# A third bank pair for two sequences' scores, an earlier pair of feed-forward turns, and newly searched instruction orders in a four-block transformer kernel

## The chip, the cores and the metric

The kernel runs on one core of a Trainium2 chip. The core has a matrix engine (PE, TensorE; its weight loads are shown as PEld), a vector engine (DVE), an activation engine (ACT), a general engine (POOL, GpSimd) and a queue engine (SP) that only issues DMAs here. Each engine executes its own instruction list strictly in order and waits on semaphores for the others. Times are microseconds of device time of one execution.

## What is computed

Sixteen sequences of 512 tokens with 128 features pass four residual blocks, each on its layer-normed input: a selective scan, a mixture of eight experts, causal attention with 16 heads, and a feed-forward block.

```python
x = x + _L0_attn_ref(_layernorm(x), ...)   # scan: h = a_t * h + bx_t, 256 channels x 16 states
x = x + _L0_ffn_ref(_layernorm(x), ...)    # residual-norm gate, top 2 of 8 experts
x = x + _L1_attn_ref(_layernorm(x), ...)   # latent q, k, v; clip, causal softmax; 16 heads
x = x + _L1_ffn_ref(_layernorm(x), ...)    # silu(w1 x)*w2 x, gelu(h1), gelu(h2), w3
```

## The kernel before

There are two phases. **Phase one** pipelines the scan, the gate with its experts, and attention over the 16 sequences: while sequence b is scanned, its predecessor is in the experts and the ones before in attention. **Phase two** does the feed-forward block for all 16 sequences. Between them every engine waits for the last residual and for the last layer-norm factor (`phase_one_over`).

Work is written as small generators, the strands: `pe_scores(b)`, `dve_g_gate(b)`, `pool_masks(b)` and so on. A strand is cut into steps by `yield`. `in_order` merges all strands of an engine by a planned time for each step: `PERIOD * b + TIMES[name][k]`, in phase one with a shift from `EDGES` for the first three and the last three sequences. The tables only fix the order in which each engine meets its instructions; they delay nothing at run time. "scores15.4" below is step 4 of sequence 15 (the last one) in the strand `pe_scores`.

The parts that the change and the prediction touch:

- PSUM has eight banks of 512 fp32 columns. Bank 0 holds the scan's input, bank 1 the scan block's projections, bank 2 the attention projections, banks 3 and 4 (one pair) the gate and the experts, banks 5 and 6 (another pair) the attention scores, bank 7 the attention values.
- `pe_scores` has 20 steps a sequence. Each writes 128 x 1024 scores into a pair, and ACT's exponential (L1092) empties it into `prob`. With one pair PE may write step s only once ACT has emptied step s - 1. The last sequence uses both pairs in turn, since the experts no longer need banks 3 and 4 then.
- `pool_masks` zeroes the part above the diagonal (L1124) before `pe_values` multiplies with the values (L1145). `pe_t_proj` makes the attention projections (L931 to L956), `pool_t_proj` adds the two rotary parts (L1018), and `sp_rows` moves the rows to where the scores read them, with 16 DMAs a sequence in two halves (L412 to L421). `pe_t_out`, `dve_t_out` end attention (L1175, L1200).
- `dve_f_first`, `pe_f_first`, `act_f_first` prepare the feed-forward inputs of sequences 0 and 1 in phase one: normalise (L1689), turn on PE into bank 1 (L471), copy the high part (L1607), subtract for the low part (L1696). `dve_f_setup` scales two small vectors and copies the five weights to another fp32 form (L1451).

```python
def dve_f_first(self, general):
    yield from self.dve_f_setup(general)
    for b in range(2):
        yield from self.dve_f_norm(b, general)
```

## Time and profile before

| | us |
|---|---|
| median of 3 runs | 1606.09 (1604.8 to 1608.68) |
| the profiled execution, its own time | 1609.73 |
| its span, first to last instruction | 1608.2 |
| mean granted PE clock | 0.959 of full speed |
| PE busy in the span | 1474.6 |
| DVE busy in the span | 1354.4 |

A busy time is the union of an engine's instructions; a row of the timeline merges neighbouring instructions of one line, gives start, length and count, and in brackets how long the engine had been idle and what ended that.

### The profile page before, as it was taken

The page shows a single profiled execution, that of the slowest core. Times are in us where ns is not written, and L with a number is a line of the kernel's source. Part 1 is how long each engine was busy: PE and PEld are TensorE (multiplying, and loading weights), DVE is VectorE, ACT ScalarE, POOL GpSimd, SP SyncE. Part 2 cuts the span into 40 slices and gives each one's busy share as a digit, 9 for nine tenths or more (in the row PEclk, how much of TensorE's full clock was granted, in tenths as well). Part 3 has the DMA queues.
Part 4 walks back from the last instruction along what each step waited for, and adds up shares of the span by engine and source line. Part 5 has one row for each costly group of instructions (what it writes and reads, how often), then busy time and mean ns, then how long its engine had stood idle before and what let it go on. Part 6 is the DMA issues. An engine that isn't in the chain of part 4 may idle for free.

```text
span 1608.2 us, 23773 instructions
## 1 busy us (share of the span) xinstructions
PE 1474.6 (92%) x7687; PEld 789.1 (49%) x7687; DVE 1354.4 (84%) x2518; ACT 1242.6 (77%) x2144; POOL 1239.7 (77%) x1219
## 2 busy tenths in 40 slices
PE   4356799999999999999999999999989899999997
PEld 2123344444444444444444444434434688788885
DVE  5999899999999999999999999995431787977774
ACT  5875699999999999999999999995545555555542
POOL 4988799999999999999999999996232355555562
PEclk8676799999999999999999999999999899999999
DMA  4000000000000000000000000002000000000000
GB/s 157 1 0 0 20 1 21 4 18 21 1 20 5 17 12 10 20 1 21 5 17 21 1 21 4 17 15 79 21 11 10 1 1 14 14 14 14 8 20 29
DMA packets 14688, 27.59 MB, mean 17 GB/s; under 512 B 3981, under 2 KB 4566, under 8 KB 14042
## 3 DMA queue, kind: packets, MB, share of 16 engines
q1 hardware_dynamic: 14554, 25.98, 5.9%
q8 instruction: 62, 1.02, 0.3%
q14 instruction: 72, 0.59, 0.1%
HBM read 9.20 MB, written 4.19 MB: 8 GB/s over the span
## 4 chain that ended last, share of the span: by engine, by line
PE 45%; DVE 28%; ACT 16%; issue 5%; DMA 4%; POOL 1%; SPq 1%; ACTq 0%; DVEq 0%; POOLq 0%
DVE state_fast L634 14%; PE bank L1076 9%; PE bank L1569 7%; PE bank L1545 7%; ACT prob_fast L1092 5%; ACT state_fast L619 4%; PE bank L747 4%; DMA stacks_fast<-parts_fast 3%; PE bank L1145 3%; ACT bank L762 3%; PE bank L505 2%; DVE chan_all_kept L570 2%; PE bank L1589 2%; DVE own_fast L892 2%; PE bank L1518 2%
## 5 line engine op out<-in xcount | busy, mean ns | idle before, releaser
L634 DVE TENSOR_TENSOR_SCAN state_fast<-state_fast,bank 128x512 f32<-128x512 f32 x512 | 592.0, 1199 | 9.6 <-ACT bank L601 5.2
L658 POOL TENSOR_TENSOR sum_fast<-sum_fast,state_fast 128x512 f32<-128x512 f32 x384 | 480.4, 1275 | 11.2 <-DVE state_fast L634 11.1
L1092 ACT ACTIVATE prob_fast<-bank 128x1024 f32<-128x1024 f32 x320 | 325.4, 1018 | 94.7 <-PE bank L1076 80.2
L1076 PE MATMUL bank<-stacks_fast 64*128 64x512 f32 (+3 forms) x2048 | 365.1, 466 | 22.6 <-DMA stacks_fast<-parts_fast 13.4
L619 ACT ACTIVATE state_fast<-chan_all_kept,neg_a_fast 128x512 f32<-128x512 f32 x512 | 344.4, 713 | 9.1 <-POOL sum_fast L652 8.6
L1076 PEld LDWEIGHTS bank<-stacks_fast 64*128 64x128 f32 x2048 | 172.2, 187 | 217.6 <-ACT prob_fast L1092 107.1
L1124 POOL TENSOR_SCALAR_AFFINE_SELECT prob_fast<-prob_fast 128x512 f32<-128x512 f32 x256 | 169.4, 674 | 121.4 <-ACT prob_fast L1092 119.3
L1145 PE MATMUL bank<-prob_fast,v_ext_fast 128*32 128x512 f32 (+3 forms) x2048 | 172.5, 442 | 5.3 <-POOL prob_fast L1124 5.3
L1758 POOL TENSOR_TENSOR cell_a_fast<-th_fast,cell_a_fast 128x512 fp32r<-128x512 f32 x64 | 99.4, 1553 | 80.3 <-ACT cell_a_fast L1630 80.3
L747 PE MATMUL bank<-we_t_fast,xnt_g_fast 128*128 128x512 f32 x256 | 141.9, 651 | 2.8 <-DVE g_prod_fast L882 2.8
L714 PE MATMUL bank<-resid_m_fast,xnt_g_fast 128*128 128x512 f32 x256 | 133.8, 631 | 6.5 <-DVE gate_fast L798 5.1
L1545 PE MATMUL bank<-cell_a_fast,w_all_fast 128*128 128x512 f32 x512 | 129.1, 395 | 0.0
L1569 PE MATMUL bank<-cell_b_fast,w_all_fast 128*128 128x512 f32 x512 | 127.8, 393 | 0.0
L1545 PEld LDWEIGHTS bank<-cell_a_fast,w_all_fast 128*128 128x128 f32 x512 | 96.7, 189 | 21.9 <-issue 0.4
L1569 PEld LDWEIGHTS bank<-cell_b_fast,w_all_fast 128*128 128x128 f32 x512 | 96.0, 188 | 21.3
L1145 PEld LDWEIGHTS bank<-prob_fast,v_ext_fast 128*32 128x32 f32 x2048 | 48.5, 108 | 113.6 <-issue 95.7
L1704 DVE SCALAR_TENSOR_TENSOR th_fast<-th_fast,bank 128x512 f32<-128x512 f32 x64 | 43.8, 684 | 65.5 <-ACT th_fast L1624 65.5
L798 DVE TENSOR_REDUCE gate_fast<-bank 128x4 f32<-128x512 f32 x128 | 83.3, 679 | 17.9 <-ACT bank L762 17.7
L652 POOL TENSOR_TENSOR sum_fast<-state_fast 128x512 f32<-128x512 f32 x64 | 86.5, 1360 | 7.1 <-DVE state_fast L634 7.1
L1774 POOL TENSOR_TENSOR cell_c_fast<-full_fast,cell_c_fast 128x512 fp32r<-128x512 f32 x32 | 41.6, 1299 | 64.9 <-DVE cell_c_fast L1737 64.9
L1630 ACT ACTIVATE cell_a_fast<-th_fast 128x512 fp32r<-128x512 f32 x64 | 40.7, 635 | 64.1 <-DVE th_fast L1713 64.0
L1624 ACT ACTIVATE th_fast<-bank,s_half_kept 128x512 f32<-128x512 f32 x64 | 43.9, 687 | 55.8 <-PE bank L1518 55.7
(218 smaller groups left out, 2632.2 us busy)
## 6 DMA issues: line engine op xcount, KB each, us to landing
stacks_fast<-parts_fast SPq DMA_DIRECT2D x128, 64.0 KB
stacks_fast<-rest_fast SPq DMA_DIRECT2D x128, 32.0 KB
out_x<-f_out_fast SPq DMA_DIRECT2D x16, 256.0 KB, 2.0
x_res_kept<-in_x SPq DMA_DIRECT2D x1, 2048.0 KB, 14.3
chan_all_kept<-in_h_t SPq DMA_DIRECT2D x2, 1024.0 KB, 9.3
x_res_kept<-in_x SPq DMA_DIRECT2D x1, 1024.0 KB, 9.9
chan_all_kept<-in_w_t SPq DMA_DIRECT2D x3, 256.0 KB, 3.0
x_res_kept<-in_x SPq DMA_DIRECT2D x2, 256.0 KB, 3.3
```

The lines of the kernel that those rows point to most:

```text
L619: act.activation(self.state(b, i)[:], self.chan(b, ct)[1], ACT.Exp, scale=self.neg_a[:, i:i + 1]).then_inc(self.a_decay.sem)
L634: dve.tensor_tensor_scan(h[:], h[:], self.banks[0][:], 0.0, ALU.mult, ALU.add).then_inc(self.v_scan.sem)
L658: pool.tensor_tensor(part[:], part[:], self.state(b, i + 1)[:], ALU.add).then_inc(self.p_sum.sem)
L714: pe.matmul(banks[3 + half][:], xnt[:, k * P:(k + 1) * P], self.resid_m[:, half * 512:(half + 1) * 512], start=True, stop=True).then_inc(s ...
L747: pe.matmul(banks[3 + e % 2][:], xnt[:, k * P:(k + 1) * P], self.we_t[:, half * 512:(half + 1) * 512], start=True, stop=True).then_inc(sel ...
L1076: ins = pe.matmul(self.scores(b, step)[:, c:c + SEQ - P * kt], rows[:, 1, h // 2, P * kt:P * kt + P], rows[:, 0, h // 2, P * kt:SEQ], star ...
L1092: act.activation(self.probs[u % 2][:, i * 1024:(i + 1) * 1024], self.scores(b, 5 * g + n)[:], ACT.Exp, scale=SCALE).then_inc(self.a_prob.sem)
L1124: pool.affine_select(out=blocks, in_=blocks, compare_op=ALU.is_ge, fill=0.0, base=0, pattern=[[0, GROUP], [1, P]], channel_multiplier=-1). ...
L1145: ins = pe.matmul(bank[32 * j:32 * j + 32, P * kt:SEQ], v_ext[:, v:v + 32], self.probs[u % 2][:, c:c + SEQ - P * kt], start=(kt == 0 and g ...
L1545: ins = pe.matmul(banks[2 + mt % 2][:], w["h1_t"][:, c:c + P], self.f_a[s][k][:, i], start=(k + i == 0), stop=(k == MT - 1 and i == parts ...
L1569: ins = pe.matmul(banks[4 + mt % 2][:], w["h2_t"][:, c:c + P], self.f_h1[s][k][:, i], start=(k + i == 0), stop=(k == MT - 1 and i == parts ...
L1758: pool.tensor_tensor(cell[:, 1], th[:], cell[:, 0].bitcast(F32), ALU.subtract).then_inc(self.p_f_lo.sem)
```

## The change

1. Banks 0 and 1 become one tensor of 1024 columns, a third pair. Sequence 14 uses two pairs for its scores (5/6 and 0/1), sequence 15 all three (5/6, 0/1, 3/4). Each step waits for the exponential as many steps back as there are pairs. The first use of banks 0/1 also waits for the low part of feed-forward input 1, which is read from bank 1.
2. `dve_f_first` does the two normalisations first and `dve_f_setup` last, and the tables put the two turns right behind the scan block of sequence 15.
3. `TIMES`, `EDGES`, `PERIOD` and `F_PERIOD` are new, `EDGES` has six more numbers a strand (a stretch of the strand's steps), and the shifts hold in phase two as well. No instruction is added or dropped.

```diff
-PERIOD, F_PERIOD = 72369, 31463
+PERIOD, F_PERIOD = 72390, 35011
...
-def place(period, name, b, k, edges):
-    shift = EDGES[name][EDGE_OF[b]] if edges and name in EDGES and b in EDGE_OF else 0
-    return period * b + TIMES[name][k] + shift
+def place(period, name, b, k):
+    times, shift = TIMES[name], 0
+    if name in EDGES and b in EDGE_OF:
+        at = EDGE_OF[b]
+        shift = EDGES[name][at] + (times[k] - times[0]) * (EDGES[name] + [0] * 6)[6 + at] / 1000
+    return period * b + times[k] + shift
...
-        self.banks = [ctx.enter_context(nc.psum_tensor(f"bank{i}", [P, 512], F32)) for i in range(3)]
+        first = ctx.enter_context(nc.psum_tensor("bank0_1", [P, 1024], F32))
+        between = ctx.enter_context(nc.psum_tensor("bank2", [P, 512], F32))
...
+        self.banks = halves(first) + [between] + halves(self.doubles[0]) + halves(self.doubles[1]) + [last]
+        self.doubles.append(first)
...
-        return self.doubles[0 if b == NSEQ - 1 and step % 2 else 1]
+        return self.doubles[self.score_rooms(b)[step % len(self.score_rooms(b))]]
+
+    def score_rooms(self, b):
+
+        return {NSEQ - 2: (1, 2), NSEQ - 1: (1, 2, 0)}.get(b, (1,))
...
-                if b == NSEQ - 1 and step == 1:
+                step, rooms = 5 * g + n, len(self.score_rooms(b))
+                if step >= rooms:
+                    pe.wait_ge(self.a_prob.sem, self.a_prob.at(b, step - rooms))
+                elif step == 0 and b:
+                    pe.wait_ge(self.a_prob.sem, self.a_prob.at(b - 1, 19 if rooms < 3 else 18))
+                elif step == 1 and b == NSEQ - 2:
+                    pe.wait_ge(split.sem, split.at(1))
+                elif step == 1:
+                    pe.wait_ge(self.a_prob.sem, self.a_prob.at(b - 1, 19))
+                elif step == 2:
                     pe.wait_ge(self.v_g_acc.sem, self.v_g_acc.at(b, 15))
...
     def dve_f_first(self, general):
-        yield from self.dve_f_setup(general)
         for b in range(2):
             yield from self.dve_f_norm(b, general)
+        yield from self.dve_f_setup(general)
```

Merging the strands by the old and by the new tables gives the orders themselves. PE around the start of sequence 14's scores, before and after:

```
before: values13.12 scores14.0 t_proj14.5 scores14.1 g_own15.0 values13.13 scores14.2 g_own15.1 g_experts15.0 t_out13.0 scores14.3 values14.0
        ... scores14.6 g_experts15.4 values14.2 scores14.7 g_experts15.5 scores14.8 g_experts15.6 g_experts15.7 scores14.9
after:  values13.12 scores14.0 scores14.1 values13.13 g_own15.0 scores14.2 g_own15.1 scores14.3 g_experts15.0 t_out13.0 g_experts15.1
        g_experts15.2 scores14.4 g_experts15.3 g_experts15.4 values14.0 values14.1 g_experts15.5 g_experts15.6 scores14.5 t_out13.1 g_experts15.7
```

Behind that, and in sequence 15:

```
PE before:   scores15.3 t_out14.0 values15.0 scores15.4 t_out14.1 values15.1 scores15.5 scores15.6 values15.2 scores15.7 scores15.8 f_first15.0 scores15.9 values15.3
PE after:    scores15.3 scores15.4 t_out14.1 values15.0 values15.1 scores15.5 scores15.6 scores15.7 values15.2 scores15.8 scores15.9 scores15.10 values15.3
DVE before:  t_norm15.0 t_proj15.0 t_proj15.1 f_first15.0 (the setup) values14.0 ... values14.3 f_first15.1 f_first15.2 t_out14.0 f_moments14.0 f_first15.3 values15.0
DVE after:   s_out15.1 f_first15.0 s_out15.2 g_norm15.0 t_proj14.0 t_proj14.1 f_first15.1 f_first15.2 g_sums15.0 ... t_out14.0 f_moments14.0 f_first15.4 (the setup) values15.0
POOL before: masks14.8 masks14.9 t_proj15.0 masks14.10
POOL after:  masks14.8 t_proj15.0 masks14.9 masks14.10
```

In a middle sequence:

```
PE before:  g_experts8.0 g_own8.1 t_out6.0 scores7.3 values7.0 g_experts8.1 t_out6.1
PE after:   g_own8.1 g_experts8.0 t_out6.0 scores7.3 t_out6.1 g_experts8.1 values7.0
DVE before: scans9.31 s_norm12.0 g_experts8.0 g_experts8.1 t_out6.0 f_moments6.0
DVE after:  scans9.31 t_out6.0 g_experts8.0 s_norm12.0 g_experts8.1 f_moments6.0
```

## Rows read from the trace of the kernel before

**Rows 1.** The page: busy time of each engine, and granted PE clock in 40 slices
```profile
PE 1474.6 (92%) x7687; PEld 789.1 (49%) x7687; DVE 1354.4 (84%) x2518; ACT 1242.6 (77%) x2144; POOL 1239.7 (77%) x1219
...
PEclk8676799999999999999999999999999899999999
```

**Rows 2.** Windows: stretch, length, busy of PE, PEld, DVE, ACT, POOL, clock, DMA
```profile
480.00:540.00 60.00, 58.87 (x330) 25.45 (x327) 58.68 (x112) 57.27 (x103) 56.85 (x59) 1.00 0.06 14
...
1140.00:1200.00 60.00, 54.18 (x338) 23.05 (x336) 22.63 (x72) 30.53 (x46) 20.79 (x29) 0.97 0.05 12
1200.00:1260.00 60.00, 50.68 (x368) 26.23 (x365) 17.06 (x52) 31.41 (x41) 14.40 (x21) 0.90 0.07 13
```

**Rows 3.** What PE waited for from 1090 to 1250: total, times, longest
```profile
PE bank L1145 <- POOL prob_fast L1124: 4.3, 3, 3.4
PE bank L1076 <- DMA stacks_fast<-parts_fast: 2.3, 2, 2.0
PE bank L1076 <- ACT prob_fast L1092: 2.0, 3, 1.1
```

**Rows 4.** Timeline of PE, late sequence 14 and the start of sequence 15
```profile
1184.37 1.13 PE L1076 MATMUL bank<-stacks_fast 64*128 64x256 f32 x8
1188.95 1.07 PE L1145 MATMUL bank<-prob_fast,v_ext_fast 128*32 128x384 f32 x16 [3.44 <-POOL prob_fast L1124]
1189.95 1.83 PE L1076 MATMUL bank<-stacks_fast 64*128 64x512 f32 x4
...
1192.89 1.49 PE L1076 MATMUL bank<-stacks_fast 64*128 64x512 f32 x4
...
1206.99 3.51 PE L1076 MATMUL bank<-stacks_fast 64*128 64x512 f32 x8 [1.98 <-DMA stacks_fast<-parts_fast]
...
1211.14 2.00 PE L1076 MATMUL bank<-stacks_fast 64*128 64x384 f32 x16
```

**Rows 5.** Windows as in rows 2, two short ones behind PE's idle times
```profile
1191.00:1195.00 4.00, 3.89 (x16) 1.00 (x14) 0.00 (x0) 2.19 (x3) 0.00 (x0) 0.67 0.00 0
...
1207.00:1211.00 4.00, 4.00 (x12) 1.51 (x12) 0.00 (x0) 1.48 (x2) 0.00 (x0) 0.57 0.33 75
```

**Rows 6.** Timelines of DVE and POOL around 1185, and all masks from 1080
```profile
1185.04 3.36 DVE L1451 CAST w_all_fast<-chan_all_kept 128x512 fp32r<-128x512 f32 x5
...
1184.39 5.09 POOL L1124 TENSOR_SCALAR_AFFINE_SELECT prob_fast<-prob_fast 128x512 f32<-128x512 f32 x3 [4.70 <-ACT prob_fast L1092]
...
1196.12 1.27 POOL L1018 TENSOR_TENSOR rest_fast<-rest_fast 68x512 f32<-68x512 f32 x1
...
L1124 POOL TENSOR_SCALAR_AFFINE_SELECT prob_fast<-prob_fast x50: 624/634/3897, 1079.5 to 1241.8; 128x512 f32<-128x512 f32 x50
```

**Rows 7.** The chain that ended last: first DMA issue of sequence 15's rows, and the landing
```profile
1197.41 0.64 SPq L412
...
1202.33 4.61 DMA stacks_fast<-parts_fast
```

**Rows 8.** Timeline of PE at the seam of the phases
```profile
1247.53 0.60 PE L471 MATMUL bank<-ident_kept,xn_f_fast 128*128 128x128 f32 x4
1250.44 0.70 PE L1518 MATMUL bank<-f_xnt_fast,w_all_fast 128*128 128x512 f32 x2 [2.31 <-DVE f_xnt_fast L1696]
```

**Rows 9.** Timelines of DVE and PE in a middle sequence, where attention of sequence 6 ends
```profile
679.37 4.54 DVE L634 TENSOR_TENSOR_SCAN state_fast<-state_fast,bank 128x512 f32<-128x512 f32 x4
...
686.09 0.68 DVE L1200 TENSOR_TENSOR x_res_kept<-bank,x_res_kept 128x512 f32<-128x512 f32 x1
...
683.02 1.07 PE L1145 MATMUL bank<-prob_fast,v_ext_fast 128*32 128x512 f32 x8
...
684.98 1.05 PE L1175 MATMUL bank<-w_o_fast,num_fast 128*128 128x128 f32 x8
```

**Rows 10.** Timeline of DVE at the first scans
```profile
29.09 4.55 DVE L634 TENSOR_TENSOR_SCAN state_fast<-state_fast,bank 128x512 f32<-128x512 f32 x4 [2.40 <-ACT bank L601]
33.56 2.29 DVE L570 SCALAR_TENSOR_TENSOR chan_all_kept<-bank,conv_w_fast,chan_all_kept 128x511 f32<-128x511 f32 x3
```

More of the change, by code:

```diff
@@ new lines @@
+    "act_f_rstd": [279204],
+    "act_f_turned": [-23966],
+    "act_g_gate": [101285, 102180, 105625, 113527, 118416],
+    "act_g_rstd": [73966],
+    "act_g_setup": [26854, 40416, 80139, 120107, 147310],
+    "act_g_squares": [83305, 84217, 89170, 89170, 92133, 92238, 96862, 98395],
+    "act_g_turned": [79107],
+    "act_g_xn": [76589],
+    "act_inputs": [-21516, 14699],
+    "act_nums": [238052, 254932, 263787],
+    "act_s_head": [-28911, -24749, -21846, -15707, -7127, -29, 8511],
+    "act_s_rstd": [-151328],
@@ new lines @@
+    "act_s_turned": [-67250],
+    "act_s_xn": [-133871],
+    "act_scores": [181763, 184612, 188853, 194201, 197184, 200424, 205025, 206941, 208116, 210722, 212767, 215596,
+        220584, 225022, 232744, 235644, 240050, 242903, 245649, 251336],
+    "act_setup": [-786538, -294800],
+    "act_t_proj": [171517, 175330, 177151],
+    "act_t_rstd": [138899],
+    "act_t_setup": [6559, 23037, 166776],
+    "act_t_turned": [146999],
+    "act_t_xn": [142130],
+    "dve_bound": [199761],
+    "dve_f_a": [18109, 22060, 26880, 34659],
@@ new lines @@
+    "dve_t_norm": [140567],
+    "dve_t_out": [267305],
+    "dve_t_proj": [156938, 163241, 184397, 189611],
+    "dve_values": [246685, 248467, 262038, 262038],
+    "pe_bound": [242319],
+    "pe_f_a": [19729, 29135, 37319, 41023],
+    "pe_f_first": [72077, 97174],
+    "pe_f_flags": [235071],
+    "pe_f_h1": [58802, 60268, 68839, 83567],
+    "pe_f_h2": [109228, 113204, 126476, 128908],
+    "pe_f_out": [168544, 178563],
+    "pe_f_turn": [-29663],
+    "pe_g_experts": [116300, 122765, 124514, 128136, 128164, 133494, 134830, 137133],
@@ new lines @@
+    "pe_setup": [-789152],
+    "pe_t_out": [262803, 264803],
+    "pe_t_proj": [154157, 161356, 168520, 174781, 178354, 181912],
+    "pe_t_setup": [-26821, -16528, 80681],
+    "pe_t_turn": [149309],
+    "pe_values": [196063, 197909, 205432, 212155, 214027, 224089, 224591, 233749, 236143, 239778, 248331, 251901,
+        252884, 256329],
+    "pool_f_a": [-42631, -42223, -37462, -26823],
+    "pool_f_h1": [4340, 10523],
+    "pool_f_h2": [54992, 67068],
+    "pool_g_sums": [122609, 122949, 126746, 127561],
@@ L241 @@
 EDGE_OF = {0: 0, 1: 1, 2: 2, NSEQ - 3: 3, NSEQ - 2: 4, NSEQ - 1: 5}
-def place(period, name, b, k, edges):
-    shift = EDGES[name][EDGE_OF[b]] if edges and name in EDGES and b in EDGE_OF else 0
-    return period * b + TIMES[name][k] + shift
+def place(period, name, b, k):
[4 more added lines that the diff above has]
+    return period * b + times[k] + shift
 def in_order(period, strands, edges=False):
-    parts = [[place(period, name, b, 0, edges), rank, 0] for rank, (name, b, _) in enumerate(strands)]
+    parts = [[place(period, name, b, 0), rank, 0] for rank, (name, b, _) in enumerate(strands)]
     for _, _, strand in strands:
@@ L261, in in_order @@
         else:
-            part[0], part[2] = place(period, name, b, k + 1, edges), k + 1
+            part[0], part[2] = place(period, name, b, k + 1), k + 1
 class Program:
```

275 lines of the change are left out of this document (139 added, 136 removed).

## Prediction

> **What bounds the kernel now.** I read the page first, for which engine is full where [rows 1]; then the windows of 60 us, to cut the run into stretches [rows 2]; then what PE waited for in the last of phase one [rows 3]; then the timelines of PE, POOL and DVE at its longest wait [rows 4 to 6].
>
> The reader is to see three stretches. Up to about 240 us the pipeline fills; the PE clock is low there [rows 1] and PE is not what limits. From 240 to 1090 us four engines are full: in the stretch shown PE is busy 58.87 of 60 us, DVE 58.68, ACT 57.27 and POOL 56.85 [rows 2]. No instruction is removed, so a new order can only fill the last one or two per cent there. The scans end near 1094 us, and from there to about 1250 us DVE falls to 22.63 and 17.06 of 60 while PE stays at 54.18 and 50.68 [rows 2]: PE, with attention for 13, 14 and 15 and the experts of 15, sets the time. Phase two is PE without gaps; the order inside it can win only at its seams, and the chain of sequence 0 at its start is ordered as before. So the money is in the tail of phase one, where PE is idle or slow.
>
> **PE's losses in the tail.** The longest wait is 3.44 us at 1188.95, a values step that waits for a mask [rows 4]. Masks take 0.63 us in the median, but one took 3.897 us, and three that started at 1184.39 took 5.09 [rows 6]. In just that stretch DVE copied the five weights, 3.36 us from 1185.04 [rows 6]. I read this as POOL being held by DVE's copies: the mask began before them and ended behind them. Behind the wait PE ran slowly: a scores step took 1.83 and one 1.49, where it takes 1.13 [rows 4], with a granted clock of 0.67 in that stretch [rows 5], that is partly at 1.2 instead of 2.4 GHz. The second loss is at 1206.99, where sequence 15's scores wait 1.98 us for their rows and the first two then take 3.51 where two take 2.00 [rows 4], at a clock of 0.57 [rows 5]. The third is 2.0 us in three waits for the exponential, the single pair of banks [rows 3].
>
> The Trainium skill has a rule for the first of these. "SBUF — State Buffer", section "Who interferes with whom", says that a DVE copy or cast can take the port pair that it shares with GpSimd, for the whole instruction, and that the other engine is blocked. The trace agrees that the mask stops while casts run, but a lock held for one instruction at a time would let the mask in between two casts; the longest of the five could hold it about 1.2 us, and the mask lost more than 3. By the page's rule alone the moved copies could cost about 1.2 us in their new place, by the row 3.3.
>
> **The change, part by part.**
>
> *The weight copies move* from between DVE's t_proj15.1 and values14.0 to behind f_moments14.0, in the middle of sequence 15's scores. The stall at 1188.95 goes: 3.44 us, and with it the slow steps, (1.83 - 1.13) + (1.49 - 1.13) = 1.06 us [rows 4]. What is late next is nothing on PE: experts 15 are over and scores 14 can run on. In their new place the copies meet masks of sequence 15. By the listed order, masks 15.0 to 15.2 need only scores up to 15.4, which PE issues before t_out14.1. DVE must first do the residual and the moments, about 2 us, before it copies. The next mask, 15.3, needs scores15.6. It would be held to about 5.4 + 0.6 = 6.0 us after t_out14.1 (2.0 of DVE work, 3.4 of copies, one mask of 0.63 [rows 6]). PE meanwhile has five more scores steps near 1.0 each (16 matmuls in 2.00, [rows 4]), one more behind them, two values steps of 1.07 [rows 4] and one shorter: about 8.5 us. So the mask has 2.5 us to spare, and I price this at nothing; if the cover is gone it costs the old price, 4.5.
>
> *Two and three pairs of banks.* With two pairs PE need not wait for the exponential of the step just before. Below, this is worth nothing, if other work already covers it; above, all of the 2.0 [rows 3]. I take 1.5, nearer the waits, since the new PE order puts pairs of scores steps next to each other, which with one pair would expose an exponential each time. The new wait for the low part of feed-forward input 1 stands at scores14.1. DVE does that part before g_gate15.0, and PE's g_own15.0 needs the whole gate and comes right behind, so it should be over by then: nothing. Everything of PE is queued behind it, though, so if it is late, each microsecond counts.
>
> *Rows of sequence 15.* POOL's rotary sum stood behind mask 14.9 and began at 1196.12 [rows 6]; SP's eight first DMAs could only start at 1197.41, were issued one by one until 1202.33, and landed 4.61 later [rows 7]. In the new order the sum precedes that mask, so that the four DMAs which need only it leave SP early (0.64 each, 2.6 us in all [rows 7]) and do not stand ahead of those for the queries and keys. Gain between 0 (PE itself arrives earlier by what it saves, and the projections are what is late) and 1.98 + (3.51 - 2.00) = 3.49 [rows 4]. I take 2.2: the wait shrinks by more than half, and a part of the slow steps remains.
>
> *Fewer changes of work on PE.* Eight scores matmuls alone take 1.13, sixteen 2.00 [rows 4], so that a joint saves up to 0.13. The new order has 6 fewer changes of strand within sequence 15 and 1 fewer between the scan's output of 15 and there: at most 0.9, I take 0.6.
>
> *The two turns.* Both now lie where PE is full. The second one cost nothing before: it ran at 1247.53, for 0.60 us, while PE was waiting for the phase to end anyway [rows 8]. Now it costs 0.6. Nothing comes back for it at the seam, because the last moments, the last layer-norm factor and ACT's table load lie in that wait too, and 2.31 us of idle before the first feed-forward matmul [rows 8] stays. DVE's and ACT's parts (1.4 and 0.6 us each) lie beside PE's work on an engine with more than half its time free [rows 2].
>
> *Orders up to 1090 us.* At the start the convolution of the second channel half (2.29 us [rows 10]) moves from between the first scans to before them, into a stretch where DVE idled 2.40 [rows 10]; ACT does more before its first decay in exchange. POOL is full behind it. Bounds: a gain of 2.7, a loss of about the same; I take 0. In the full stretch I take 0 as well; the loss possible there is a rival.
>
> **Sum.** 3.44 + 1.06 + 1.5 + 2.2 + 0.6 - 0.6 = 8.2 us. The profiled execution's own time was 1609.73, 1.5 above its span, and 3.6 above the median of the runs. It becomes 1601.5; the median, 1606.09, becomes 1597.9, say 1598. With all upper ends and the start's gain the saving is 3.44 + 1.06 + 2.0 + 3.49 + 0.9 + 2.7 - 0.6 = 13.0 plus some of the other 0.9 of mask waits [rows 3], near 1592; with nothing but the moved copies it is 4.5 - 0.6 = 3.9, 1602.
>
> **Rivals.**
>
> 1. *The copies hold POOL again*, now in sequence 15. For it: the same 3.36 us of copies, and masks are dense there. Against it: the 2.5 us to spare and up to three pairs. Price 4.5, time 1606.1 - 3.7 = 1602.4. The page's rule would make it about 1599, since only one cast would hold the mask; the trace so far speaks for the longer hold.
> 2. *More pairs buy nothing*, the change doesn't do what it says: PE is busy with one thing or another, and the rows of sequence 15 are late because their projections are. For it: outside the stall and the rows, only 2.0 us in 160 are waits for ACT [rows 3]. Only the copies count: 1602.
> 3. *A wait in every middle sequence*, the one that ends on the other side. DVE now does t_out before the first expert product, right behind the last scan. That scan ends at 683.91, while PE ended L1175 at 686.03 [rows 9]. The new PE order pulls it ahead of one values step (1.07 [rows 9]) and one expert step of about the same, so to about 684.0. The margin is nil. If PE comes 1 us later than this, DVE, and with it the scans, loses 1 us in each of some 13 sequences: 1606.1 - 8.2 + 13 = 1610.9. From 0.6 us on it eats the gain; above 1.0 it is slower by over 0.3%. Against it: PE and DVE are coupled, and what waits in one step may be regained in the next.
> 4. *The order finds more*: the 1 to 3 us of idle in each 60 us of the full stretch [rows 2] shrink by 0.5 us a sequence beside the tail's gain: 1606.1 - 8.2 - 6.5 = 1591.4.
>
> **How the numbers follow.** The forecast has a chance of 0.52, with a range of its own from 1592 to 1602. Rival 1 has 0.10, rival 2 has 0.15, rival 3 has 0.13 (half of it slower by over 0.3%), rival 4 has 0.10. The range 1591 to 1605 takes in the forecast, rivals 1, 2 and 4 and the mild part of 3, and leaves out somewhat under 0.2. A measurement of this kernel can tell about 0.3% (4.8 us) from no change. Faster by more than that means below 1601.3: the forecast but for a little, and rival 4, together 0.62. Slower, above 1610.9, 0.08. The rest, 0.30, is rivals 1 and 2 and the mild 3.
>
> **What the new profile would show.** No mask above 1 us that PE waits for, though one in sequence 15 may be long; the copies near the place where the residual of 14 is added. A granted clock of 1.00 from 1180 to 1205 us. The wait at the first scores of 15 under 1 us. The time from the last scan to the seam some 8 us shorter, all other stretches the same within 2 us. I am wrong if the last scan itself comes later (rival 3), if a values step of sequence 15 waits 3 us for POOL (rival 1), if scores14.1 waits for the low part, or if PE's waits in the tail have only moved to another step with the same sum.

## The result, and the profile after

The change made the kernel slower: 1628.48 us median (1626.14 to 1630.48, 4 runs) beside 1606.74 us for the kernel before in the same session (1604.8 to 1608.68, 4 runs). The ratio is 1.0135, 95% interval 1.0116 to 1.0154. The forecast was 1598, range 1591 to 1605. The profiled execution took 1627.94 us, with a span of 1626.3.

Line numbers of the new kernel are higher by 61 to 70: L634, the scan, is L695; L658 is L719; L817 is L878; L1124 is L1194; L1518 is L1588.

The page has the first sign, beside [rows 1]. The clock line is much the same, but DVE is busy 42.8 us longer with the same 2518 instructions:

```profile
PE 1481.4 (91%) x7687; PEld 795.5 (49%) x7687; DVE 1397.2 (86%) x2518; ACT 1242.2 (76%) x2144; POOL 1235.5 (76%) x1219
...
PEclk8577799999999999999999999999999799999999
```

Windows of the new kernel, columns as in [rows 2]:

```profile
480.00:540.00 60.00, 57.09 (x321) 25.30 (x320) 58.88 (x114) 55.37 (x100) 54.63 (x59) 0.97 0.03 9
...
1140.00:1200.00 60.00, 59.86 (x369) 28.42 (x371) 28.83 (x90) 36.12 (x60) 17.53 (x30) 1.00 0.20 62
1200.00:1260.00 60.00, 56.18 (x457) 27.03 (x449) 12.06 (x34) 36.62 (x49) 19.25 (x26) 1.00 0.06 14
```

In the middle, DVE alone is as busy as before while PE, ACT and POOL are each 1.8 to 2.2 us less busy. In the tail PE is fuller than before (59.86 and 56.18 of 60 for 54.18 and 50.68) and its clock is whole. So the tail did what it was meant to do, and the loss is where the prediction had put a zero.

The span can be cut at three events: the end of the last scan, the end of the last attention residual, the first feed-forward product. Each row gives the length of a part in us; the last two columns are experiments told below, the kernel after with two outputs in PSUM, and the same with the old orders in phase two. The parts are rounded so that each column adds up to its span.

| part of the span | before | after | PSUM outputs | and old phase two |
|---|---|---|---|---|
| to the end of the last scan | 1094.0 | 1121.6 | 1084.2 | 1085.4 |
| from there to the end of the last residual | 154.4 | 140.8 | 142.2 | 140.9 |
| from there to the first product of phase two | 2.0 | 1.8 | 1.8 | 1.8 |
| phase two | 357.8 | 362.1 | 364.4 | 358.3 |
| span | 1608.2 | 1626.3 | 1592.6 | 1586.4 |

After less before: +27.6, -13.6, -0.2 and +4.3, together +18.1.

**Where the 27.6 us arise.** A residual addition that runs once a sequence measures the period. It is L682 before and L743 after, and these are its twelve records in the steady stretch (shortest, median and longest ns, first and last start):

```profile
L682 DVE TENSOR_TENSOR x_res_kept<-bank,x_res_kept x12: 658/672/674, 293.8 to 1051.6; 128x512 f32<-128x512 f32 x12
```

```profile
L743 DVE TENSOR_TENSOR x_res_kept<-bank,x_res_kept x12: 659/670/693, 286.8 to 1075.9; 128x512 f32<-128x512 f32 x12
```

Eleven periods: (1051.6 - 293.8) / 11 = 68.89 us before, (1075.9 - 286.8) / 11 = 71.74 after, 2.85 more in each sequence, 31.3 in all. The first of these records stands 7.0 us earlier than before and the stretch behind the last of them to the last scan's end is 3.3 us longer, which leaves the 27.6. Of the 7.0 some 4 to 5 may be chance: in two kernels with the old orders in phase one (experiments 9 and 10) this first record stands at 288.3 and 290.0. The groups of DVE by line and shape tell which instruction grew. Before:

```profile
L858 DVE TENSOR_SCALAR gate_fast<-kept_all_kept 128x4 f32<-128x4 f32 x16 | 3.9, 242 | 0.5
L817 DVE TENSOR_SCALAR gate_fast<-gate_fast 128x32 f32<-128x32 f32 x16 | 2.8, 178 | 0.5
```

and after:

```profile
L878 DVE TENSOR_SCALAR gate_fast<-gate_fast 128x32 f32<-128x32 f32 x16 | 32.4, 2024 | 0.0
...
L919 DVE TENSOR_SCALAR gate_fast<-kept_all_kept 128x4 f32<-128x4 f32 x16 | 11.5, 718 | 0.5
```

L878 is the first step of the gate, a max of 128x32 numbers with a constant. It took 178 ns on the mean and now takes 2024, and its median is 2830. It does not wait for a semaphore; it is *running* for 2.8 us. The timelines of POOL, DVE and ACT in one middle sequence show beside what. Before:

```profile
665.33 1.26 POOL L658 TENSOR_TENSOR sum_fast<-sum_fast,state_fast 128x512 f32<-128x512 f32 x1
666.59 0.18 DVE L817 TENSOR_SCALAR gate_fast<-gate_fast 128x32 f32<-128x32 f32 x1
...
667.29 1.22 POOL L1124 TENSOR_SCALAR_AFFINE_SELECT prob_fast<-prob_fast 128x512 f32<-128x512 f32 x2 [0.70 <-ACT prob_fast L1092]
```

and after:

```profile
674.18 2.50 POOL L719 TENSOR_TENSOR sum_fast<-sum_fast,state_fast 128x512 f32<-128x512 f32 x2
...
675.07 2.82 DVE L878 TENSOR_SCALAR gate_fast<-gate_fast 128x32 f32<-128x32 f32 x1
...
676.64 1.21 POOL L1194 TENSOR_SCALAR_AFFINE_SELECT prob_fast<-prob_fast 128x512 f32<-128x512 f32 x2
677.92 0.23 ACT L830 ACTIVATE gate_fast<-gate_fast 128x32 f32<-128x32 f32 x1 [2.61 <-DVE gate_fast L878]
```

Before, POOL had one sum to do and then stood idle for 0.70 us, and the small max ran there. After, it is issued 0.89 us into a train on POOL (operations that follow each other without a gap), two sums of 1.26 us and two masks of 0.62 (each row merges two), and it ends at 677.89, 0.04 behind the end of the train at 677.85. The same stands in 11 consecutive sequences, from 316 to 1033 us. ACT's logarithm waits for it, and the square behind that, and with that TensorE. Waits from 240 us to the end of the stretch (total, times, longest) of PE and ACT:

```profile
PE bank L1004 <- ACT squares_fast L1038: 24.2, 11, 2.2
```

```profile
ACT gate_fast L830 <- DVE gate_fast L878: 28.8, 11, 2.6
```

In the middle of the kernel before neither wait is listed. The granted clock follows: the window from 480 to 540 us, which holds such a wait of 2.2 us, has 0.97 where it was 1.00 [rows 2], so PE ran a part of it at 1.2 and not at 2.4 GHz.

### The profile page after: what moved, and what is told of

Read it like the earlier page. It is cut to its first block, busy times and chain, and to the rows that moved or that the text cites. A ratio compares the mean times of both kernels' runs of the same rounds, so it can differ in the third digit from the quotient of the medians.

```text
span 1626.3 us, 23772 instructions
## 1 busy us (share of the span) xinstructions
PE 1481.4 (91%) x7687; PEld 795.5 (49%) x7687; DVE 1397.2 (86%) x2518; ACT 1242.2 (76%) x2144; POOL 1235.5 (76%) x1219
## 4 chain that ended last, share of the span: by engine, by line
PE 36%; POOL 24%; issue 17%; DVE 15%; ACT 7%; DMA 1%; SPq 0%; POOLq 0%; ACTq 0%; DVEq 0%
POOL sum_fast L719 9%; PE bank L1146 6%; PE bank L1639 6%; PE bank L1615 6%; DVE state_fast L695 5%; POOL prob_fast L1194 4%; PE bank L1215 3%; PE bank L808 3%; POOL sum_fast L713 2%; PE bank L1659 2%; PE bank L1588 1%; ACT prob_fast L1162 1%; PE bank L1593 1%; POOL g_prod_fast L966 1%; DVE gate_fast L859 1%
## 5 line engine op out<-in xcount | busy, mean ns | idle before, releaser
L695 DVE TENSOR_TENSOR_SCAN state_fast<-state_fast,bank 128x512 f32<-128x512 f32 x512 | 590.3, 1198 | 2.7 <-ACT bank L662 1.9
L719 POOL TENSOR_TENSOR sum_fast<-sum_fast,state_fast 128x512 f32<-128x512 f32 x384 | 481.0, 1278 | 23.4 <-DVE state_fast L695 23.4
L1146 PE MATMUL bank<-stacks_fast 64*128 64x512 f32 (+3 forms) x2048 | 360.8, 462 | 18.0 <-ACT prob_fast L1162 8.4
L1194 POOL TENSOR_SCALAR_AFFINE_SELECT prob_fast<-prob_fast 128x512 f32<-128x512 f32 x256 | 169.5, 676 | 131.9 <-ACT prob_fast L1162 131.8
L1215 PE MATMUL bank<-prob_fast,v_ext_fast 128*32 128x512 f32 (+3 forms) x2048 | 178.7, 461 | 2.5 <-POOL prob_fast L1194 2.4
L1828 POOL TENSOR_TENSOR cell_a_fast<-th_fast,cell_a_fast 128x512 fp32r<-128x512 f32 x64 | 90.6, 1417 | 117.4 <-ACT cell_a_fast L1700 117.2
L1215 PEld LDWEIGHTS bank<-prob_fast,v_ext_fast 128*32 128x32 f32 x2048 | 52.9, 114 | 128.6 <-issue 86.7
L1736 ACT ACTIVATE full_fast<-bank,sh_kept 128x512 f32<-128x512 f32 x64 | 43.8, 690 | 61.0 <-PE bank L1639 39.2
L1700 ACT ACTIVATE cell_a_fast<-th_fast 128x512 fp32r<-128x512 f32 x64 | 40.3, 630 | 64.1 <-DVE th_fast L1783 63.9
L775 PEld LDWEIGHTS bank<-resid_m_fast,xnt_g_fast 128*128 128x128 f32 x256 | 44.8, 193 | 75.3 <-DVE gate_fast L859 45.5
L823 ACT ACTIVATE bank<-bank 128x512 f32<-128x512 f32 x128 | 71.3, 576 | 10.3 <-PE bank L775 10.2
```

The lines of the kernel that those rows point to most:

```text
L695: dve.tensor_tensor_scan(h[:], h[:], self.banks[0][:], 0.0, ALU.mult, ALU.add).then_inc(self.v_scan.sem)
L719: pool.tensor_tensor(part[:], part[:], self.state(b, i + 1)[:], ALU.add).then_inc(self.p_sum.sem)
L775: pe.matmul(banks[3 + half][:], xnt[:, k * P:(k + 1) * P], self.resid_m[:, half * 512:(half + 1) * 512], start=True, stop=True).then_inc(s ...
L1146: ins = pe.matmul(self.scores(b, step)[:, c:c + SEQ - P * kt], rows[:, 1, h // 2, P * kt:P * kt + P], rows[:, 0, h // 2, P * kt:SEQ], star ...
L1194: pool.affine_select(out=blocks, in_=blocks, compare_op=ALU.is_ge, fill=0.0, base=0, pattern=[[0, GROUP], [1, P]], channel_multiplier=-1). ...
L1215: ins = pe.matmul(bank[32 * j:32 * j + 32, P * kt:SEQ], v_ext[:, v:v + 32], self.probs[u % 2][:, c:c + SEQ - P * kt], start=(kt == 0 and g ...
```

## The experiments

The theory (A) is that one held operation, L878, costs the whole loss. The rivals are that the order lengthens the chain of a sequence in itself and the held operation fills a wait that is there anyway (B), and that the train holds whatever operation comes at that place (C).

**1. The same orders, with two small outputs in PSUM.**

```diff
-        dve.tensor_scalar(ss, ss, LN_MIN, None, ALU.max)
+        dve.tensor_scalar(sp, ss, LN_MIN, None, ALU.max)
-        act.activation(ss, ss, ACT.Ln)
+        act.activation(ss, sp, ACT.Ln)
-        dve.tensor_scalar(col(4), kept, KEPT_MIN, None, ALU.max)
-        dve.reciprocal(col(5), col(4))
+        dve.tensor_scalar(self.banks[4][:, 160:164], kept, KEPT_MIN, None, ALU.max)
+        dve.reciprocal(col(5), self.banks[4][:, 160:164])
```

> The kernel after with its orders untouched; only the two small tensor_scalar operations of the gate (L878, the max of 128x32, and L919, the max of 128x4) write their results to PSUM in place of SBUF, and their readers read them there. Theory A (the loss of 27.5 us up to the end of the scans comes from this one operation, which in the new order is issued while GpSimd runs a train of operations with both operands in SBUF, and waits until the train has a gap): L878 falls from a mean of 2024 ns to under 0.4 us, the period of a sequence from 71.7 towards 68.9 us, and the time from 1628 to between 1595 and 1608. Rival B (the order itself makes the chain of a sequence longer, and the long operation only fills a wait that is there anyway): L878 is short, but the time stays within 4 us of 1628. Rival C (the train holds whichever operation of VectorE comes at that place): another VectorE operation takes the 2.8 us, and the time stays above 1620.

1594.18 us median (1589.88 to 1602.64, 7 runs), ratio to before 0.9931 (0.9905 to 0.9956): 34.3 us less than the kernel after, and faster than before. The timeline of POOL and DVE at the same place:

```profile
656.64 2.53 POOL L719 TENSOR_TENSOR sum_fast<-sum_fast,state_fast 128x512 f32<-128x512 f32 x2
...
657.53 0.19 DVE L878 TENSOR_SCALAR bank<-gate_fast 128x32 f32<-128x32 f32 x1
```

The operation is issued 0.89 us into the same train, to the hundredth, and takes 0.19 us. The period:

```profile
L743 DVE TENSOR_TENSOR x_res_kept<-bank,x_res_kept x12: 659/670/691, 286.0 to 1039.3; 128x512 f32<-128x512 f32 x12
```

(1039.3 - 286.0) / 11 = 68.48 us, 3.26 less than after and 0.41 less than before. Theory A holds (the time is even 1 us below its range), B and C fall: up to the last scan the order is sound, and nothing else is held in its stead. The 3.26 us are more than the 2.65 that L878 lost each time; the slow products behind PE's wait are the likely rest, which these runs do not split off.

**2. Only the first of the two.** As experiment 1, with L919 and its reader left in SBUF.

> The kernel after with only the first of the gate's two operations (L878, max of 128x32) writing to PSUM; the second (L919, max of 128x4, held for 0.93 us on the median) stays in SBUF. Theory A (the chain goes through L878 alone, as ScalarE waits for it and not for L919): 1594 to 1596. Rival (the second one's 8 us of held time count too): 1598 to 1603.

1594.19 us (1590.66 to 1595.94, 4 runs), ratio 0.9916 (0.9893 to 0.9940). L919 costs nothing that these runs can tell: no other engine waits for it. One operation of 128x32 makes the whole difference.

**3. The same edit in the kernel before.**

> The kernel before with the edit of the gate's two operations to PSUM alone (L817 and L858 of before). Theory (the edit pays only where the order puts the operation into a train of GpSimd; before, L817 took 178 ns on the mean): no change, 1605 to 1609. Rival (the edit speeds up something else as well, which would mean that the 34 us it won from the kernel after are not all the held operation's): 1600 or less.

1604.60 us (1603.63 to 1607.03, 10 runs) beside 1607.78, ratio 0.9985 (0.9974 to 0.9996). A trace of a gain, 2.4 us by the ratio and just below the range that the theory gave, against 34 in the kernel after: the edit pays where the order brings the operation into a train. Where the 2.4 us come from is open; L817 itself takes 192 ns on the mean here, for 178, and L858 166 for 242.

**4. Another form of the operation, still in SBUF.**

```diff
-        dve.tensor_scalar(ss, ss, LN_MIN, None, ALU.max)
+        dve.scalar_tensor_tensor(ss, ss, LN_MIN, ss, ALU.max, ALU.max)
```

> The kernel after with its orders untouched; L878, the max of 128x32 (a tensor_scalar, SBUF to SBUF, that took 2.8 us wherever a train of GpSimd operations ran), becomes a scalar_tensor_tensor with the same result (the max with the same number, then the max with itself), still all in SBUF. Theory 1 (the operation is held because its operands all lie in SBUF): it still takes 2.8 us in most sequences and the time stays at 1628. Theory 2 (only the form with one tensor operand is held, a form with two tensor operands is not): it takes about 0.2 us and the time is that of the kernel with the PSUM outputs, 1594, or a little more for L919, which is left in SBUF here.

1630.60 us (1627.84 to 1631.69, 4 runs), ratio 1.0139 (1.0122 to 1.0156), and the operation by its line:

```profile
L878 DVE SCALAR_TENSOR_TENSOR gate_fast<-gate_fast x16: 165/2854/3010, 110.7 to 1166.2; 128x32 f32<-128x32 f32 x16
```

Held just the same. The Trainium skill has the rule for this, in "SBUF — State Buffer", section "Who interferes with whom": copies, casts and tensor_scalar can take the port pair that DVE shares with GpSimd, a DVE operation with two SBUF inputs meets GpSimd's reads there, and whoever issues first has the pair while the other is blocked. The traces agree that the form with two SBUF inputs is held (2854 ns on the median) and the tensor_scalar that writes SBUF (2830). For a tensor_scalar that writes PSUM the section refers to conditions on the operands told elsewhere; here it was not held (186 ns on the median).

**5. A move of three steps in DVE's order.** The two value drains go ahead of the last sums of the gate and a copy goes behind its first step, in the kernel after with all operations in SBUF.

```diff
-    "dve_s_head": [-57363, -42459, -10464, -3050],
+    "dve_s_head": [-57363, -40400, -10464, -3050],
-    "dve_values": [246685, 248467, 262038, 262038],
+    "dve_values": [246200, 246200, 262038, 262038],
```

> The kernel after, all operations as they are (the gate's too, in SBUF); in VectorE's order of every sequence three small steps are moved: the two value drains come ahead of the last two sums of the gate, and the copy of the scan's head behind the first step of the gate. L878 is then issued up to 1.2 us earlier than in the kernel after; GpSimd's order is untouched. Theory A (the operation is held until the train on GpSimd has its first gap, whenever it is issued): it ends where it ended, so its own time grows to 3.5 to 4 us, and the time stays at 1628, give or take 3. Rival (it is held for one GpSimd operation at most, and takes 2.8 us for some cause of its own): 2.8 us or less. Third case (it now comes ahead of the train, into the gap before it): about 0.2 to 0.5 us, and 1594 to 1600.

1627.71 us (1626.68 to 1628.96, 4 runs), ratio 1.0132 (1.0113 to 1.0151). The timeline of the same sequence:

```profile
674.54 2.50 POOL L719 TENSOR_TENSOR sum_fast<-sum_fast,state_fast 128x512 f32<-128x512 f32 x2
...
675.14 3.12 DVE L878 TENSOR_SCALAR gate_fast<-gate_fast 128x32 f32<-128x32 f32 x1
...
677.00 1.23 POOL L1194 TENSOR_SCALAR_AFFINE_SELECT prob_fast<-prob_fast 128x512 f32<-128x512 f32 x2
```

The train before the operation shifted too, so that it came only 0.29 us earlier in the train (0.60 us in, and not 0.89), and it took 0.30 us longer: 3.12 for 2.82. It again ended 0.03 us behind the train. Its duration is set by the train's end and not by the operation, as A says, though the size I had given, 3.5 to 4, was too large, as the rival's, 2.8 or less, was too small. One sequence, though, went otherwise:

```profile
961.17 2.50 POOL L719 TENSOR_TENSOR sum_fast<-sum_fast,state_fast 128x512 f32<-128x512 f32 x2
961.88 0.60 DVE L878 TENSOR_SCALAR gate_fast<-gate_fast 128x32 f32<-128x32 f32 x1
```

Here it ended at 962.48, 0.06 us behind the joint of the two sums (961.17 + 1.25), and that period was 68.9 us and not 71.6. So it can come in between two operations of a train; in the ten other sequences from 317 to 1031 us it did not.

**6. DVE's old order in the middle, the rest new.**

```diff
+def is_old(name, b):
+    part = name.split("_", 1)[1]
+    return name.startswith("dve_") and 3 <= b <= 12 and not part.startswith("f_")
 def place(period, name, b, k):
+    if is_old(name, b):
+        shift = OLD_EDGES[name][EDGE_OF[b]] if name in OLD_EDGES and b in EDGE_OF else 0
+        return OLD_PERIOD * b + OLD_TIMES[name][k] + shift
```

> The kernel after, with VectorE's order alone taken back to that of the kernel before for sequences 3 to 12; TensorE, ScalarE, GpSimd and SyncE keep the new orders. Theory A: the max of 128x32 (L878) then comes behind two value drains as before, meets no train on GpSimd, and is back near 180 ns in those ten sequences; the period there falls by 2 to 2.85 us, and the time by 20 to 27 us, to 1601 to 1608. Rival B (the loss is in the orders of the other engines): the time stays within 4 us of 1628. Rival D (an old VectorE order beside new ones on the others makes waits of its own): slower than 1630.

1627.77 us (1627.25 to 1630.81, 4 runs), ratio 1.0130 (1.0113 to 1.0147): no gain at all in the whole time, which is what B forecast. The trace says why. In the middle of the stretch that was turned back, from 443 to 858 us, the gate's first step (L1022 here) and the residual addition (L887) read:

```profile
L1022 DVE TENSOR_SCALAR gate_fast<-gate_fast x6: 647/648/656, 472.7 to 817.6; 128x32 f32<-128x32 f32 x6
```

```profile
L887 DVE TENSOR_TENSOR x_res_kept<-bank,x_res_kept x7: 670/673/693, 443.3 to 857.6; 128x512 f32<-128x512 f32 x7
```

The period is (857.6 - 443.3) / 6 = 69.05 us, 2.7 less than after: A's figure, where the order is the old one on both sides. The operation itself took 0.65 us and not the 0.18 that A expected, since in POOL's new order it does meet a train. At the two seams between the tables the engines no longer meet: the periods there are 78.9, 72.6 and 74.7, and 71.4, 75.2 and 75.2. Over the first seam alone, from 217 to 443 us, PE waited 8.0 us in two waits for the gate's products. What six sequences won the seams lost. B is not borne out, but the time of this run alone could not have told. The operation is held only to the joint of two sums here, though the train goes on without a gap (two sums, two masks):

```profile
540.89 2.50 POOL L863 TENSOR_TENSOR sum_fast<-sum_fast,state_fast 128x512 f32<-128x512 f32 x2
541.54 0.65 DVE L1022 TENSOR_SCALAR gate_fast<-gate_fast 128x32 f32<-128x32 f32 x1
...
543.33 1.23 POOL L1338 TENSOR_SCALAR_AFFINE_SELECT prob_fast<-prob_fast 128x512 f32<-128x512 f32 x2
```

It came in at the first joint in all nine sequences from 327 to 889 us (0.27 to 0.94 us). In the next but one, at 1034 us, which has the new order of DVE again, it was held for 2.81 us, to the end of a train of the same four operations.

**7. Old orders for sequences 0 to 12 and phase two, new ones for 13 to 15.**

```diff
+    if part in PHASE_TWO:
+        return True
+    if part in ("f_first", "bound", "weights"):
+        return False
+    return b <= 12
```

> The kernel after (its third pair, its place of the copies, its two early inputs), with the orders of the kernel before for all work of sequences 0 to 12 and for phase two, and the new orders for sequences 13 to 15 alone. Theory (the ledger of the two profiles adds up part by part: +27.5 us up to the last scan, -13.5 in the tail, +4.3 in phase two): only the tail's part stays, so 1606.7 - 13.5 = 1593, give or take 4 for the seam between the tables. Rival (the tail gained 13.5 us only because it began 27.5 us late, with other engines ahead by then): the gain shrinks to the 8 us of the prediction or less, 1599 to 1607. Seen in the stretch from the last scan to the last t_out: 140 us by the theory, 150 or more by the rival.

1637.79 us (1634.42 to 1642.44, 4 runs), ratio 1.0198 (1.0171 to 1.0225): a miss by 45 us, neither the theory nor the rival. At the seam, from 980 to 1160 us, PE waited (total, times, longest):

```profile
PE bank L1373 <- POOL prob_fast L1352: 9.6, 4, 3.5
PE bank L1304 <- ACT prob_fast L1320: 8.4, 11, 1.7
```

The last periods are 87.0 and 79.5 us, and the last scan ends at 1132.3. The two tables did not join in the middle of the run, so the parts of the ledger can't be added by cutting in time. The stretch from the last scan to the last residual took 143.4 us, though, near the 140 of the theory. As the last scan was late here too, this does not answer the rival; experiment 1 does, whose tail is 142.2 us with the last scan at 1084.2. Phase two, whose orders are planned by themselves, can be exchanged: here it took 357.4 us from its first product, with the old orders.

**8. Phase two alone turned back**, on top of experiment 1.

```diff
+def is_old(name, b):
+    return name.split("_", 1)[1] in PHASE_TWO
```

> The kernel after with the gate's PSUM outputs (1594.2), and for phase two, whose orders are planned apart from phase one's, the orders of the kernel before. In the profiles phase two, from its first product to the end of the span, is 357.8 us in before, 356.4 and 357.4 in two kernels with the old orders there, and 362.1 and 364.4 with the new ones. Theory (the new phase-two orders cost what the profiles say): 1594.2 - 6.6 = 1587.6, between 1586 and 1590. Rival (phase two is longer because its first 16 us run at half clock after the new tail, whatever its orders): 1592 to 1596.

1588.03 us (1587.93 to 1594.98, 4 runs), ratio 0.9887 (0.9862 to 0.9911). The last group of products on the first weights, of experiment 1 (L1588) and of this kernel (L1734), first and last start:

```profile
L1588 PE MATMUL bank<-f_xnt_fast,w_all_fast x128: 391/397/797, 1228.2 to 1542.2; 128*128 128x512 f32 x128
```

```profile
L1734 PE MATMUL bank<-f_xnt_fast,w_all_fast x128: 388/395/794, 1228.1 to 1537.3; 128*128 128x512 f32 x128
```

Both start at the same time and the old order is 4.8 us ahead at the last of them. The time is as the theory had it. The phase-two orders alone are worth less than these 6 us, though: experiment 1's phase two, 364.4 us, is the longest of the kernels with the new orders there, the others took 361.1 to 362.2, and with the old orders it took 356.4 to 358.3. That is about 4 us, the rest is scatter. This version beats both kernels: 18 us (1.1%) below before by the ratio, and 40 below the median of after.

**9. The copies alone**, in the kernel before.

```diff
-    "dve_f_first": [165839, 196471, 196471, 218728, 404306],
+    "dve_f_first": [196471, 196471, 218728, 404306],
+    "dve_f_setup": [207000],
```

> The kernel before with one thing changed: the two copies of feed-forward weights to bf16 (3.36 us each in VectorE's order, which held GpSimd's mask of sequence 15 and so TensorE for 3.44 us) come behind the moments of sequence 14. By the prediction's term: 3.44 for the wait and 1.06 for the slow clock behind it, so 1606.7 - 4.5 = 1602.2. Rival (the next thing is late by as much, or the copies hold another mask): 1604 to 1608, with a new TensorE wait of 1 us or more on GpSimd or VectorE in the tail.

The expectation misnames two things: the copies are the five of [rows 6], to fp32r and 3.36 us together, and the masks that they held are those of sequence 14.

1601.29 us (1597.28 to 1605.09, 10 runs), ratio 0.9972 (0.9959 to 0.9985), which is 4.5 us (2.4 to 6.6), the predicted term. The profile is that of the fastest of the ten, and its part up to the last scan, where nothing was changed, is 5.1 us shorter as well. In it the tail is 148.4 us for 154.4, and the longest wait of PE for a mask there is 0.6 us, from 3.4 [rows 3].

**10. The second input early as well**, on top of experiment 9.

```diff
-    "act_f_first": [205950, 257282],
+    "act_f_first": [205950, 212000],
-    "dve_f_first": [196471, 196471, 218728, 404306],
+    "dve_f_first": [196471, 196471, 218728, 222000],
-    "pe_f_first": [249821, 419927],
+    "pe_f_first": [249821, 256000],
```

> The kernel before with the two weight copies behind the moments of sequence 14 (1601.3 alone), and the second of the two feed-forward inputs turned in the tail, ahead of the last sequence's output, and not behind it. By the prediction's term: 0.6 us less, 1600.7, as 0.60 us of turns and part of a 2.31 us wait leave the seam. Rival (phase two cannot start sooner than some 2 us behind the last residual, whatever is ready): no change, 1601, and the first product of phase two still starts 1.8 to 2.0 us behind the end of the last residual addition.

1609.26 us (1606.18 to 1613.49, 10 runs), ratio 1.0013 (0.9997 to 1.0029): by the ratios 7 us slower than experiment 9, which neither the term nor the rival had. My place for the turn was bad (the tail is 157.8 us for 148.4), and the seam gave nothing back (timeline of PE):

```profile
1222.45 1.12 PE L472 MATMUL bank<-ident_kept,xn_f_fast 128*128 128x128 f32 x4 [5.24 <-DVE xn_f_fast L1690]
...
1249.16 0.70 PE L1519 MATMUL bank<-f_xnt_fast,w_all_fast 128*128 128x512 f32 x2 [2.59 <-issue]
```

PE stood 5.24 us before the turn, as DVE had not yet made its input, and ran slowly behind it. The first product of phase two begins 1.9 us behind the end of the last residual (1247.3), where before it was 2.0 [rows 8] with the second input still to be turned. So the seam does not depend on it; in this the rival was right.

**11. The score pairs as before, in the new orders**, on top of experiment 1.

```diff
-        return {NSEQ - 2: (1, 2), NSEQ - 1: (1, 2, 0)}.get(b, (1,))
+        return {NSEQ - 1: (1, 0)}.get(b, (1,))
```

> The kernel after with the gate's PSUM outputs (1594.2), but the score pairs as in the kernel before: one pair for sequence 14, two for sequence 15, and each product's wait on its pair as before; orders unchanged. By the prediction's term for the pairs (1.5 us, and 2.2 for the earlier rows of sequence 15, which the orders give and not the pairs): 1596. Rival 1 (the orders of the tail are planned for three pairs and the products stand in line without them): 1600 or more. Rival 2 (the pairs buy nothing): 1593 to 1595.

1615.74 us (1611.22 to 1620.38, 4 runs), ratio 1.0054 (1.0036 to 1.0072): by the ratios 20 us above experiment 1, so rival 1 holds. PE's waits from 1085 to 1265 us:

```profile
PE bank L1142 <- ACT prob_fast L1158: 17.9, 19, 2.1
```

where it waits 0.2 us in experiment 1. The new order puts scores steps side by side, and each one needs a pair of its own.

**12. Two pairs each.** As experiment 1, with `NSEQ - 1: (1, 2)`.

> The kernel after with the gate's PSUM outputs (1594.2) and two pairs of banks for the scores of sequence 14 and two for 15, where it has two and three; with one and two it took 1615.7. Theory (what is worth 20 us in the new tail is the second pair of sequence 14, the third pair of 15 little, as the ScalarE exponentials bound it): 1594 to 1597. Rival (the third pair is what the orders of the last sequence need): 1602 or more, with TensorE's waits for the exponentials behind 1160 us.

1596.64 us (1594.56 to 1598.25, 4 runs), ratio 0.9936 (0.9915 to 0.9957). The third pair of sequence 15 is worth 2.2 us of the tail (144.4 for 142.2), within the scatter of the times. The second pair of 14 carries the rest.

## Why the prediction was wrong

**The step that failed is "Orders up to 1090 us", "In the full stretch I take 0 as well".** It measured +27.6 us. I counted waits and instructions per engine, and a new order that removes no instruction then seemed able only to win or lose idle time. But the duration of some operations on DVE depends on what POOL runs beside them, and the new order moved a 178 ns operation with its operands in SBUF into a train on POOL, 11 times at 2.8 us. The row to see it by was in the profile: in [rows 6] a mask of 0.63 us takes 3.897 beside DVE's casts. I used it for the copies alone and did not ask the same of each small DVE operation in SBUF that the order moved.

**The rule of the Trainium skill was read too narrowly.** I weighed it for the copies and found it too mild for the mask. The same rule names L878, a tensor_scalar within SBUF, from the other side: there POOL was first and DVE waited.

**Rival 3 had the right sign and place, and the wrong mechanism.** It priced a wait of DVE for PE before the residual addition. That wait is 5.3 us in ten waits after, and 11.1 in twelve in experiment 1 at a period of 68.48 us, so it costs nothing. The time it gave, 1610.9, was short by 18.

**The copies**: 3.44 + 1.06 = 4.5 us, measured 4.5 (2.4 to 6.6, experiment 9). In the profiles the tail lost 6.0: PE's waits for masks fell from 4.3 to 1.0 us and its busy time by 3.2, so the slow products probably cost more than the 1.06 of the two rows. Their new place was not free in the new order, though. Timelines of DVE, POOL and PE of the kernel after:

```profile
1231.63 3.36 DVE L1521 CAST w_all_fast<-chan_all_kept 128x512 fp32r<-128x512 f32 x5
```

```profile
1231.90 4.18 POOL L1194 TENSOR_SCALAR_AFFINE_SELECT prob_fast<-prob_fast 128x512 f32<-128x512 f32 x2 [1.81 <-ACT prob_fast L1162]
```

```profile
1235.54 0.64 PE L1215 MATMUL bank<-prob_fast,v_ext_fast 128*32 128x256 f32 x8 [1.22 <-POOL prob_fast L1194]
```

Rival 1's hold is there (two masks in 4.18 us), and PE's scores ahead of it cover all but 1.22 us of it. A price of 1.2 would have been right, between the nothing of the sum and the 4.5 of the rival. That the prediction names 1.2 as well, for a hold by one cast alone, is luck: the hold was about 3.5 us and the cover took the rest.

**The rest of the tail**: pairs 1.5, rows 2.2, fewer changes 0.6, turns -0.6, together 3.7 us; measured 13.6 - 4.5 = 9.1. The waits went as predicted: PE waits 0.2 us for the exponential from 1125 to 1262 us, and not at all for the rows of sequence 15 or for the low part, at a clock of 1.00 in both windows. That is 4.1 us less than the 2.0 and 2.3 of [rows 3], for 3.7 in the sum. What was too small is PE's busy time in the tail, which fell by 7.7 us (windows from the last scan to the last residual, before and after, columns as in [rows 2]):

```profile
1094.00:1248.40 154.40, 142.98 (x943) 64.88 (x939) 53.24 (x164) 80.98 (x118) 52.45 (x77) 0.98 0.11 30
```

```profile
1121.60:1262.40 140.80, 135.32 (x937) 63.15 (x933) 53.32 (x165) 80.19 (x117) 52.51 (x76) 1.00 0.11 33
```

The groups of PE's instructions in these windows say what it is. The 360 scores products are busy 59.7 us for 63.9, at the clock of 1.00 for 0.98. Eight products of an output projection and two expert products, 2.4 us together, now come ahead of the last scan's end, so they left this part of the ledger and were not saved. The rest are small amounts in many groups. Experiments 11 and 12 show something else, that the new order needs the pairs it was laid out for: with one pair for 14 it is 19 us slower than with two (experiments 11 and 12, by the ratios). What the pairs would bring in the old order no run shows. Rival 2, that only the copies count, is not borne out by these waits.

**The seam**: predicted unchanged, measured 2.0 and 1.9 us. Experiment 10 agrees.

**Phase two**: taken as unchanged; it cost 4.3 us after, and 6.1 between experiments 1 and 8, of which some 2 are scatter. Its orders were new and I had not gone through them. In the kernel with the PSUM outputs PE waits for the tanh step of DVE 5.3 us in six waits, and 3.6 in three with the old order. That is 1.7; the rest I have not placed.

**The sum again, with what the runs give**: 1606.7 + 27.6 - 13.6 - 0.2 + 4.3 = 1624.8 against 1628.5. The parts are of the profiled executions: that of before took 1609.7, 3.0 above its median, and that of after 1627.9, 0.5 below its own, which makes 3.5 of the 3.7 between.

## What to carry to other kernels

Where DVE and POOL are both nearly full, a small DVE operation within SBUF can take as long as POOL's train beside it, if it is of a form that is held; here these were a tensor_scalar and a scalar_tensor_tensor. In a new order compare the mean time of each line as well as the waits, and ask what POOL runs where such an operation is issued. If its result is wanted on the chain, try letting it write to PSUM when a corner is free; here that one edit of a 128x32 operation was worth 34 us of 1628. An order and the buffers it was laid out for are to be changed together (experiment 11), and half an order can't be tested by joining it to another in the middle of a pipeline (experiments 6 and 7); at the seam of the phases, where all engines meet, it could (experiment 8).

## What the runs showed of the hardware

A held DVE operation of 178 ns took 2.82 us beside four POOL operations, two of 1.26 us and two of 0.62. The Trainium skill's section "Who interferes with whom" ("SBUF — State Buffer") says that the engine that is first has the pair for the whole instruction. That alone would let DVE in at the first joint, after 0.36 us in the row at 675.07. In the kernel after it came in only behind the last one in all 11 middle sequences, 0.04 us behind it. In the next sequence of the same kernel, at 1102.50, it came in at the first joint of a train of seven or more and took 0.30 us. So it did in nine sequences in a row of experiment 6, and once in the middle of experiment 5. How far into POOL's first operation it is issued doesn't decide it: it was held to the end when issued 0.46 to 0.98 us in, and let in when issued 0.37, 0.65, 0.71 and 1.01 us in. Nor do the records of POOL's operations, which start 0.03 to 0.09 us before the one ahead ends in both cases. Why DVE wins the joint in one case and loses it in the other is open, and no run here tells it.

Writing the output of this operation to PSUM was enough to free it, with its input still in SBUF (0.19 us, 0.89 us into the same train). A form with two SBUF inputs was held as long (2854 ns on the median) as the form with one (2830).

Not every DVE operation within SBUF is held. In the kernel after the reciprocal of 128x4 numbers that ends the same stretch of the gate (L891) is issued 0.11 to 0.23 us into a mask on POOL in the 11 middle sequences, and takes what it takes elsewhere. Its 16 records, and the rows of POOL and DVE in one sequence:

```profile
L891 DVE RECIPROCAL gate_fast<-gate_fast x16: 166/168/178, 114.3 to 1171.2; 128x4 f32<-128x4 f32 x16
```

```profile
680.99 0.69 POOL L1194 TENSOR_SCALAR_AFFINE_SELECT prob_fast<-prob_fast 128x512 f32<-128x512 f32 x1 [3.14 <-ACT prob_fast L1162]
681.10 0.17 DVE L891 RECIPROCAL gate_fast<-gate_fast 128x4 f32<-128x4 f32 x1
```
